# Attention and expert kernel on one core: transposed input, own banks for batch 0, one head sum, other queues for some transfers, rows scattered into the result

## The reference

```python
qkv = x @ Wqkv                                   # layer 1
q, k = apply_rope(q), apply_rope(k)
q = q / sqrt(sum(q * q, axis=-1) + 1e-06)        # the same for k
attn = softmax(q @ k.T / 4)
x = layernorm(x + (attn @ v) @ Wo + bo)

h = x + msa(layernorm(x, ln1), w_qkv, w_proj)    # layer 2
logits = layernorm(h, ln2) @ gate_w + gate_b     # h + expert(argmax(logits))
y = gelu(t @ w1[e]) @ w2[e]                      # t = layernorm(h, ln2)
x = layernorm(x + h + y)
```

## Time and profile before

| what | us |
|---|---|
| median of three runs (1433.34 to 1435.84) | 1433.45 |
| profiled execution, own time | 1429.04 |
| its span, first to last instruction | 1427.1 |
| PE, DVE, ACT, POOL busy | 1279.5 (90% of the span), 792.0, 919.6, 311.5 |
| first score matmul | 62.59 |
| expert tiles, first transpose to last scatter | 1108.61 to 1409.17 |

### The profile page before, as it was taken

How to read it: one execution, slowest core, us unless ns; L and a number is a source line. 1 busy time by engine, 2 the same in 40 slices (tenths; PEclk the granted TensorE clock), 3 DMA queues, 4 the chain that set the end, 5 groups by cost and what they waited for, 6 DMA issues and landing times. The chain is left out here.

```text
span 1427.1 us, 21029 instructions
## 1 busy us (share of the span) xinstructions
PE 1279.5 (90%) x7238; PEld 687.5 (48%) x7238; DVE 792.0 (55%) x1815; ACT 919.6 (64%) x1617; POOL 311.5 (22%) x247
## 2 busy tenths in 40 slices
PE   3599999999999898999999999999961899999993
PEld 1233443443443333444434443444331898989993
DVE  3333554554552677787878787878823333433341
ACT  0277777777777565676666666766640477767773
POOL 5122233233232110222222222212122011111111
PEclk9799999999999999999999999999995899999997
DMA  7231331331432121214131313131357111111113
GB/s 194 88 99 46 127 114 56 127 114 55 127 114 92 57 90 60 81 54 104 46 104 47 105 46 109 51 96 61 134 183 244 53 49 53 56 54 52 52 56 133
DMA packets 103496, 127.87 MB, mean 90 GB/s; under 512 B 7168, under 2 KB 91008, under 8 KB 103264
## 3 DMA queue, kind: packets, MB, share of 16 engines
q1 hardware_dynamic: 71088, 79.06, 17.6%
q10 hardware_dynamic: 27872, 33.95, 7.5%
q0 software_dynamic: 4432, 13.52, 3.1%
HBM read 51.51 MB, written 28.46 MB: 56 GB/s over the span
## 5 line engine op out<-in xcount | busy, mean ns | idle before, releaser
L665 ACT ACTIVATE w_space<-bank 128x512 f32<-128x512 f32 x1024 | 564.4, 601 | 288.3 <-PE bank L450 275.4
L868 DVE TENSOR_REDUCE negm<-bank 128x1 f32<-128x512 f32 x512 | 334.3, 685 | 97.2 <-PE bank L482 93.6
L450 PE MATMUL bank<-w_space 96*128 96x512 bf16 (+1 forms) x1024 | 354.7, 385 | 12.4 <-DMA w_space<-work_space 9.8
L467 PE MATMUL bank<-w_space 128*32 128x512 f32 x2048 | 275.2, 610 | 0.6 <-ACT w_space L674 0.6
L450 PEld LDWEIGHTS bank<-w_space 96*128 96x128 bf16 (+1 forms) x1024 | 93.6, 99 | 278.2 <-ACT w_space L665 204.3
L482 PE MATMUL bank<-w_space 96*128 96x512 bf16 x512 | 197.3, 385 | 16.4 <-DVE negm L868 7.6
L638 PE MATMUL bank<-w_space,work_space 128*128 x624 | 141.4, 380 | 0.0
L511 PE MATMUL bank<-work_space,wqkv_sb 128*128 128x512 f32 x256 | 123.0, 603 | 7.5 <-DVE w_space L995 4.8
L638 PEld LDWEIGHTS bank<-w_space,work_space 128*128 128x128 f32 x624 | 115.5, 190 | 14.2
L1222 POOL TENSOR_TENSOR work_space<-w_space,work_space 128x1024 bf16<-128x1024 f32 x32 | 68.3, 2136 | 226.1 <-ACT work_space L713 145.7
L1278 POOL DMA_INDIRECT out_rows<-rows_sb,work_space x39 | 37.5, 963 | 267.6 <-DVE rows_sb L1172 267.6
(11 more groups left out here) (131 smaller groups left out, 1451.5 us busy)
## 6 DMA issues: line engine op xcount, KB each, us to landing
w_space<-work_space SPq DMA_DIRECT2D x384, 128.0 KB
w_space<-in_w_dram ACTq DMA_DIRECT2D x16, 1024.0 KB, 8.5
work_space<-rows_dram SPq DMA_DIRECT2D x39, 256.5 KB, 2.6
work_space<-in_x_dram ACTq DMA_DIRECT2D x16, 512.0 KB, 3.8
x_dram<-xo SPq DMA_DIRECT2D x16, 256.0 KB, 3.2
h_dram<-row_sb SPq DMA_DIRECT2D x16, 256.0 KB, 2.2
work_space<-h_dram ACTq DMA_DIRECT2D x8, 512.0 KB, 3.9
work_space<-x_dram ACTq DMA_DIRECT2D x8, 512.0 KB
```

The lines of the kernel that those rows point to most:

```text
L450: nc.tensor.matmul(bank[:, :], k_stack[0:rows, b % 2, HEADS_AT_ONCE * g + j, kt * P:(kt + 1) * P], q_stack[0:rows, b % 2, HEADS_AT_ONCE * ...
L467: last = nc.tensor.matmul(pv_bank[VW * j:VW * (j + 1), :], v_aug[:, b % 2, at:at + VW], probs[:, q % PROBS, j, :], start=(kt == 0), stop=( ...
L665: nc.scalar.activation(probs[:, q % PROBS, j, :], st_bank(b, c)[0][:, :], ACT.Exp, scale=SCALE).then_inc(exps, 1)
L868: ve.tensor_reduce(negm[:, c % TT, c // TT:c // TT + 1], mx_ring.bank(b, (g, c))[:, :], axis=AX.X, op=ALU.max, negate=True).then_inc(mx_ri ...
```

## The change

- The host also passes the input transposed (`x_t`). Layer 1 loads that, into two alternating buffers, and its T0 and T1 tasks are gone. In layer 1 the four projections and sq stand three or four chunks earlier, the later steps of q one to three chunks later, those of k one to six.
- The squares of a head are added on DVE first (new tasks aq, ak), so that nq and nk are one matmul each.
- In batch 0 every projection task has a bank of its own, and k's cosine products have a buffer of their own (`trig_of`).
- PE starts when the q and k columns of the first weight and the input are there. Those two loads come first on SP and ACT. Cosine and sine go on ACT's queue. Other constants are waited for where they are used.
- The ones in `k_stack` come by DMA. The zero rows for `rows_dram` (9 DMAs of 256 KB) are written in stage 2, not at the start.
- In batch 0, ACT issues the 12 copies of `k_stack` while SP issues those of `q_stack`.
- In layer 1 the copy of the attention output (`group_out`) stands one chunk earlier on ACT.
- The ten late weight loads move from ACT's queue to SP's.
- `tile_out` stands ahead of `weights_of` in DVE's loop over expert tiles.
- POOL scatters into the result itself, with a bounds check that drops padding rows; the eight closing copies are gone.

```diff
 PROJECTED = (
-    dict(T0=(0, 0), T1=(0, 2), qA=(1, 3), qB=(2, 2), kA=(3, 3), kB=(4, 2), sq=(4, 2), nq=(5, 3),
-         sk=(6, 0), uq=(6, 2), hq=(6, 3), nk=(7, 0), lq=(7, 1), uk=(8, 1), hk=(8, 2), lk=(9, 0),
+    dict(qA=(0, 3), qB=(1, 2), kA=(2, 3), kB=(3, 3), sq=(3, 3), aq=(4, 3), nq=(6, 0), sk=(6, 1),
+         uq=(7, 1), ak=(7, 2), hq=(7, 2), lq=(8, 0), nk=(8, 2), uk=(9, 2), hk=(9, 3), lk=(10, 1),
          V0=(12, 0), V1=(14, 0)),
+COPY_AFTER = (1, 2)
-        out_rows = dram("out_rows", [BATCH * T + P, D])
+        out_rows = out.rearrange("b t d -> (b t) d")
-        p_ring = Ring("proj", [psum[4]], sem)
+        p_ring = Ring("proj", [psum[i] for i in (4, 0, 1, 2, 3, 5, 6, 7)], sem)
-                            p_ring.add(b, name, 0)
+                            p_ring.add(b, name, 0 if b else len(p_ring.uses))
+        def trig_of(b, qk):
+            return probs[:, 0, :, :] if b == 0 and qk else trig
 # PE
-            pe.wait_ge(consts_in, 16 * N_FIRST)
-            pe.wait_ge(consts_set, N_CONST_OPS)
+            pe.wait_ge(w_in, 16 * KD)
-                    for k in range(2):
-                        last = nc.tensor.matmul(bank[:, :], head_sum_sb[:, :], sq[:, k, :],
-                                                start=(k == 0), stop=(k == 1))
+                    last = nc.tensor.matmul(bank[:, :], head_sum_sb[:, :], sq[:, 0, :],
+                                            start=True, stop=True)
 # ACT
+                elif name == "lk" and b == 0:
+                    stack_copies(act, b, 1)
-                    if n == last + 2 and q == 6:
-                        load_weights(0, (2, 3, 6, 7), [(scores, CHUNKS * (last + 1)),
-                                                       (dispatched, 16 * TT * (BATCH - 1))])
-                        load_weights(1, (0, 1, 2, 3, 4), [(pv_done, QUADS * (last + 1))])
-            load_weights(1, (5,), [o_ring.full(last, "GT1")])
 # DVE
+                if name in ("aq", "ak"):
+                    dve.wait_ge(sq_done, 2 * b + ("qk".index(name[1]) + 1))
+                    ve.tensor_tensor(sq[:, 0, :], sq[:, 0, :], sq[:, 1, :], ALU.add
+                                     ).then_inc(sq_added, 1)
             for j in range(1, TILES):
+                if j > 1:
+                    tile_out(j - 2)
                 if j + 1 < TILES:
                     weights_of(j + 1)
                     tile_in(j + 1)
-                if j > 1:
-                    tile_out(j - 2)
                 tile_sum(j - 1)
 # POOL
-            pool.memset(k_stack[STACK:STACK + NEG, :, :, :], 1.0).then_inc(pool_set, 1)
-                    o_sb[:, s, :], None).then_inc(out_stored[s], 16)
+                    o_sb[:, s, :], None, bounds_check=BATCH * T - 1, oob_is_err=False
+                    ).then_inc(out_stored[s], 16)
 # SP
+            last = 2 * BATCH - 1
+            load_weights(sp, 0, (2, 3, 6, 7), [(scores, CHUNKS * (last + 1)),
+                                               (dispatched, 16 * TT * (BATCH - 1))])
+            load_weights(sp, 1, (0, 1, 2, 3, 4), [(pv_done, QUADS * (last + 1))])
+            load_weights(sp, 1, (5,), [o_ring.full(last, "GT1")])
-            for b in range(BATCH):
-                sp.dma_start(out[b], out_rows[b * T:(b + 1) * T, :]).then_inc(out_done, 16)
```

138 lines of the change are left out of this document (81 added, 57 removed).

## The result

The changed kernel takes **1375.78 us** (median of 4 runs, 1374.35 to 1376.77) against 1433.39 for the kernel before in the same comparison (1432.81 to 1435.84): a ratio of 0.959, 95% interval 0.9574 to 0.9607. That is faster, by 57.6 us where 77 were forecast, and above the range of 1341 to 1371. In a later comparison, unaltered, it took 1376.4 (0.960, 0.9583 to 0.9617). The profiled execution took 1376.04, with a span of 1374.0 us where the span before was 1427.1, so 53.1 us are to be found between the two traces. The other 4.5 lie in the yardstick: the profiled execution of the kernel before ran 4.4 under its own median, that of the changed kernel at its median.

What follows compares the result with a forecast made beforehand. PE was taken as the limit where it is waited for. Gains of 23.5, 24, 13.5, 1 and 15 sum to 77 off 1429.04, giving 1352.0; the median's 4.4 more makes 1356 us, range 1341 to 1371.

Steps and rivals of the forecast that it cites:

- The stages of layer 1: Seven layer 1 stages: 18.1 us less PE work and 6.3 of nk's waits for ACT gone; 24 us (12 to 26).
- there PE is the limit: Layer 1 stage: PE idle only 1.04 of 53.5 us while ACT is busy 41.6, so saved PE work counts.
- The start: Start of the kernel up to the first score: it comes at 39 instead of 62.59, 23.5 us earlier (17 to 27).
- I take the issue, not the transfer, as the limit: Batch 0's stack copies: 189 GB/s against 379 elsewhere, so a second issuing queue helps; first score at 39.
- two queues that copy no faster than one: Rival for batch 0's stack copies: first score at 43.7, kernel near 1361; within a shared chance of 0.19.
- The passage: From attention to the experts: weight loads on SP let R2 start 15.1 earlier, less 1.6 contention; 13.5 us (6 to 15.1).
- The end: Behind the last scatter: the eight closing copies go, saving 15 us (13 to 15.5).
- about 0.5 of closing stays: End of the span: of 15.5 us from 1411.59 to 1427.1, about 0.5 remains without the copies.
- The tiles: Expert tiles: output row 1.18 us earlier, 1.04 lost if POOL's scatter waits for DVE's weight copy; 1 us (0 to 9.5).
- layer 1 pays half: Rival: stack copies or another new wait in the projection chain take back 14 us in layer 1; 1370, chance 0.12.
- the scatter is not held: Rival in the expert tiles: DVE's copy does not delay POOL's scatter, all 12 row waits go; 1348, chance 0.25.
- the start or the passage pays less: Rival: transfers hold the passage, paying 6 (1364), or stack copies gain nothing from two queues (1361); chance 0.19.

Runs made afterwards that it cites:

- l_two_sums: Changed kernel with the head sum made of two matmuls again and the add on DVE gone: 1384.78 us, ratio 0.9666.
- l_half_square: Changed kernel with ACT squaring only half the values of q and k in layer 1: 1370.72 us, against 1376.40 for the changed kernel beside it.
- l_spread: Changed kernel with k's square, its add and TP1 moved one to three chunks later in layer 1: 1374.07 us, ratio 0.9583.
- s_k_split: Changed kernel with k's 12 stack copies of batch 0 shared, six from ACT and six from SP behind q's: 1377.16 us, ratio 0.9612.
- x_out_behind: Changed kernel with a tile's output row made behind the next tile's weight copy and input copy again: 1383.39 us, ratio 0.9648.

## Why the prediction was wrong

The five places were right, and the total came 20 us short in the medians (1375.8 against 1356) and 24 between the two traces (53.1 against 77). Two terms account for most of it; the others follow.

- **The stages of layer 1, 24 us forecast, 11.6 measured** (10.0 in the second profile). The step that failed is "there PE is the limit": the sum has PE's saved work and nk's wait in full and no term for a new wait on ACT. The prediction cites ACT's 12 free us, of 53.5, only where it puts the earlier copy at nothing. PE's saved work was sized well (2.41 a stage against 2.58) and nk's wait went. But ACT's free time is an average over the stage. In the chunks around nq, sk and TP1 it has none, and there PE met 10.1 us of new waits in seven stages: 18.1 + 6.3 - 10.1 = 14.3, and 14.1 came by batch 8's first projection. l_two_sums and l_half_square each took 5.9 of the waits away, one by slowing PE, one by relieving ACT. The change also put nq and sk one chunk nearer to TP1 and the copy one chunk earlier; l_spread says that the places matter a little (0.26 us a stage), and no run puts the old ones back. The rest of the shortfall, 2.5 us in one profile and 4.2 in the other, lies between there and batch 8's routing. PE waited longer there for row maxima (8.6 against 7.4) and at a k projection (1.79 against 1.31); the mean granted clock was 0.97 and 0.96 against 0.97. That is not all of it, and I didn't test it.
- **The start, 23.5 forecast, 18.5 measured.** Loads, projections and the last split came nearly as worked out (33.91 against 33.4). The failed step is "I take the issue, not the transfer, as the limit". The rival "two queues that copy no faster than one" put the score at 43.7; it came at 44.06. The row that should have warned me was there: 189 GB/s in the stack copies. I read it against the 379 GB/s of other transfers as room to spare, but another kind of transfer need not reach that rate, and one queue, two queues and s_k_split's mixture all moved the copies at the same pace. The copies' share of 0.54 is half of the 1.06 to 1.10 seen in the weight loads, and the packet records of the changed kernel show the same: most often 8 packets in flight at once from 36 to 40 us, 16 or 17 from 1054 to 1058. So the copies look as if they used half of the DMA engines, and a second queue adds none. Each copy writes 8 rows of the stack; no run changes that, so the reason stays open. The Trainium skill (DMA: Bandwidth & Descriptors, Issuing engines are not separate DMA queues) says that a second issuing engine saves only issue time. The runs agree (24 copies in 16.03 us from one queue, 16.45 from two), and I had overruled it without a row that measured it.
- **The passage, 13.5 forecast, 9.8 measured.** R2's 15.1 came. The contention was the mis-sized term: 1.6 forecast, 5.0 measured. I shared the rate by halves, over a short overlap (2.8 us for the whole, 1.6 taken). The scatters lost more than a half share would take; with three loads fewer ahead of them they lost 0.5. Whether they stood behind the earlier loads or shared with them at a lower rate, no run separates.
- **The end, 15 forecast, 10.8 measured.** The copies cost 11.2, not 15, because "about 0.5 of closing stays" was wrong: 5.0 us lie between the last scatter's landing and the end of the span, while only 2.1 lay behind the closing copies' traffic. The trace of before held one end only, and I took its 15.5 us as nearly all the copies' own.
- **The tiles, 1 forecast, 3.9 measured.** The hold exists: 1.57 us for the scatter under the weight copy, 0.96 to 0.98 without. I had it take back 1.04 of the 1.18 by which the output moves. But the copy starts 0.34 behind the output row, not 0.57 (1206.24 to 1206.58), and POOL's instruction begins under it, 0.86 behind; it grows by 0.59, with 0.71 of the copy still to run (1207.10 to 1207.81). So 0.6 is lost, and half a microsecond a tile is left, enough for most of the waits. The rule that the prediction drew on (the Trainium skill, SBUF — State Buffer, SBUF: two separate sides: while a fp32 copy within SBUF holds the port pair, GpSimd can't write descriptors) agrees with it: POOL's issue grew by 0.59, nearly the 0.71 that was left of the copy, and in x_out_behind, where no copy lies there, not at all (0.98).
- **Rivals.** That layer 1 pays half for "another new wait" had 0.12 and was the case, at 1370 by itself. That the scatter is not held, 0.25, was not. That the start or the passage pays less had 0.19 and was true of both. The range treated these as alternatives, and they came together. The rival's 14 us for layer 1 and the start's 5, both on the forecast of 1356, would have made 1375. That this is near the 1375.8 measured is in part luck: layer 1 lost 12.4, passage and end lost 7.9 more, and the tiles gained 2.9 beyond the forecast.

## What to carry to other kernels

When work comes off the limiting engine, check the next engine's load in the same few chunks, not over the stage; a stage that is 20% free on average can have none where the saved work lay. Before giving transfers a second queue, compare the rate they reach, and their DMA share, with those of the same kind of transfer, not with the best in the trace. And when several independent ways of being paid less exist, let the range hold two or three of them at once.
